# Causal mask of the first scores added by VectorE in PSUM instead of by matmuls; later pairs' q evacuated by ScalarE instead of VectorE

## The reference

```python
xn = layernorm(x)                                   # x: 8 x 2048 x 1024, one sequence per core
q, k, v = split(xn @ W_attn + b_attn)               # 16 heads of 64
att = (q @ k.T) / sqrt(64) / temperature
att = where(k_pos <= q_pos, att + slope[h] * (k_pos - q_pos), -inf)
y = softmax(att) @ v
h = silu(xn @ wg.T / 127) * (xn @ wu.T / 127)       # 3072 wide
out = x + (y @ W_proj + b_proj) + h @ wd.T / 127
```

## Time and profile before

| | |
|---|---|
| median of 3 runs | 1139.33 us (1138.94 to 1139.5) |
| profiled execution | 1137.8 us |
| its span on the slowest core (core 2) | 1136.2 us; the other cores 1131.2 to 1134.5 us |
| mean granted TensorE clock | 0.997 on that core |
| TensorE, VectorE, ScalarE, GpSimd busy | 1082.9, 628.3, 479.5, 332.8 us |

### The profile page before, as it was taken

The page is one execution under the profiler, slowest core; times in us unless marked ns, Lnnn a source line. Parts: engine busy times, 40 slices in busy tenths (PEclk is TensorE's granted clock), DMA queues, the critical chain, the costliest instruction groups (busy, mean ns, idle before and its releaser), DMA issues.

```text
span 1136.2 us, 23969 instructions; the slowest of 8 cores (1131.2 to 1136.2 us)
## 1 busy us (share of the span) xinstructions
PE 1082.9 (95%) x7270; PEld 535.8 (47%) x7270; DVE 628.3 (55%) x1254; ACT 479.5 (42%) x869; POOL 332.8 (29%) x529
## 2 busy tenths in 40 slices
PE   2898899999999999999999999999999999999998
PEld 1444355545545555454554554455554344444443
DVE  4531867776776786787777678677882100001100
ACT  2443345655655565555565556556666200000000
POOL 7210112423332342233333233223333422222220
PEclk9999999999999999999999999999999999999999
DMA  8448032433412433143331213113521552525222
GB/s 191 141 93 169 16 62 67 79 72 71 84 41 65 84 81 67 39 85 67 71 57 33 64 38 67 32 33 69 173 61 54 203 190 74 185 74 185 74 77 72
DMA packets 57070, 98.34 MB, mean 87 GB/s; under 512 B 23292, under 2 KB 43909, under 8 KB 55862
## 3 DMA queue, kind: packets, MB, share of 16 engines
q0 software_dynamic: 7872, 35.66, 16.1%
q1 hardware_dynamic: 46178, 52.65, 15.7%
q10 hardware_dynamic: 2900, 8.51, 1.9%
HBM read 90.50 MB, written 27.26 MB: 104 GB/s over the span
## 4 chain that ended last, share of the span: by engine, by line
PE 87%; DVE 6%; issue 3%; DMA 2%; ACT 1%; POOL 1%; DVEq 0%; ACTq 0%; POOLq 0%; SPq 0%
PE ps_gu L752 25%; PE ps_dn L914 15%; PE ps_s L843 10%; PE ps_t L824 10%; PE ps_m L732 9%; PE ps_y L862 5%; PE ps_dn L909 5%; PE ps_t L792 5%; DVE cm L577 3%; PE ps_s L846 1%; DMA xstage<-xin 1%; DVE hst L513 1%; DMA tile_s<-tiles 1%; DVE qx L607 1%; DVE st L525 0%
## 5 line engine op out<-in xcount | busy, mean ns | idle before, releaser
L694 ACT ACTIVATE pt<-ps_t 128x512 bf16<-128x512 f32 (+1 forms) x576 | 328.6, 575 | 297.9 <-PE ps_t L824 283.2
L577 DVE TENSOR_REDUCE cm<-ps_s 128x1 f32<-128x512 f32 (+3 forms) x640 | 377.1, 607 | 136.4 <-PE ps_s L843 81.6
L752 PE MATMUL ps_gu<-xnT,wubuf 128*128 128x512 bf16 x768 | 261.5, 378 | 2.3 <-DVE hst L513 2.3
L752 PE MATMUL ps_gu<-xnT,wgbuf 128*128 128x512 bf16 x768 | 261.8, 378 | 1.2 <-ACT kst L638 1.2
L843 PE MATMUL ps_s<-kx,qx 67*128 67x512 bf16 (+3 forms) x640 | 215.6, 347 | 12.9 <-DVE cm L577 9.2
L824 PE MATMUL ps_t<-qx,kx 104*128 104x512 bf16 (+3 forms) x640 | 212.6, 348 | 5.2 <-DVE qx L607 4.4
L914 PE MATMUL ps_dn<-wdres,hb 128*128 128x512 bf16 x768 | 168.5, 379 | 0.0
L443 POOL TENSOR_SCALAR th_s<-th_s 128x512 f32<-128x512 f32 x96 | 59.4, 619 | 364.6 <-ACT th_s L646 364.0
L862 PEld LDWEIGHTS ps_y<-Vt,pt 128*128 128x128 bf16 x2176 | 121.5, 97 | 79.3 <-issue 0.9
L627 DVE SCALAR_TENSOR_TENSOR outsb<-ps_dn,xres 128x512 f32<-128x512 f32 x32 | 20.7, 687 | 205.1 <-PE ps_dn L914 205.1
L862 PE MATMUL ps_y<-Vt,pt 128*128 128x65 bf16 x2176 | 134.1, 193 | 0.0
(11 more groups left out here) (75 smaller groups left out, 707.9 us busy)
## 6 DMA issues: line engine op xcount, KB each, us to landing
h_sc<-hst SPq DMA_DIRECT2D x96, 128.0 KB, 1.9
hb<-h_sc SPq DMA_DIRECT2D x4, 3072.0 KB, 14.3
xstage<-xin SPq DMA_DIRECT2D x16, 512.0 KB, 6.2
xres<-xin POOLq DMA_DIRECT2D x16, 512.0 KB, 4.9
out<-outsb ACTq DMA_DIRECT2D x15, 512.0 KB, 3.0
wgbuf<-wg_r POOLq DMA_DIRECT2D x12, 512.0 KB, 5.3
wubuf<-wu_r POOLq DMA_DIRECT2D x12, 512.0 KB, 7.9
wd_sc<-wd_r POOLq DMA_DIRECT2D x12, 512.0 KB, 7.7
```

What stands on the lines that cost most here:

```text
L577: e.tensor_reduce(cm[:, c0:c0 + 1], ps_s[:, s % 2 * 512:s % 2 * 512 + w], AX.X, AluOpType.max, negate=True).then_inc(sem["v_mx"], 1)
L694: e.activation(pt[t % NPT][:, 0:w], ps_t[:, t % 2 * 512:t % 2 * 512 + w], AF.Exp).then_inc(sem["a_e"], 1)
L752: mm = e.matmul(ps_gu[:, r // 8 * 512:r // 8 * 512 + 512], w[:, w0:w0 + 128], xnT[:, dc * T + tb * 512:dc * T + tb * 512 + 512], start=(dc ...
```

## The change

The mask matmuls go. VectorE instead adds `mask_s` to the last 128 columns of a diagonal group, in place in PSUM, and reduces the group when that addition has told of its end through a new semaphore `v_ms`. The evacuation of q for pairs 1 to 7 moves from VectorE (one `tensor_scalar`) to ScalarE (one `activation`, same scale and bias); pair 0 stays. SyncE and TensorE wait for ScalarE's semaphore `a_q` there.

```diff
@@ block.vector, reduces of a step
                     e.wait_ge(sem["p_s"], s + 1)
+                    if part == b:
+                        d0 = s % 2 * 512 + w - 128
+                        e.tensor_tensor(ps_s[:, d0:d0 + 128], ps_s[:, d0:d0 + 128], mask_s[:, 0:128],
+                                        AluOpType.add).then_inc(sem["v_ms"], 1)
+                        e.wait_ge(sem["v_ms"], 4 * n + i + 1)
                     e.tensor_reduce(cm[:, c0:c0 + 1], ps_s[:, s % 2 * 512:s % 2 * 512 + w], AX.X,
                                     AluOpType.max, negate=True).then_inc(sem["v_mx"], 1)
@@
-                if M is not None and M[0] == "qk" and M[2] and M[1] % 2 == 0:
-                    evac_q(M[1] // 8 + 1, M[1] % 8 // 2)
@@ block.scalar
+            def evac_q(p, tc):
+                e.wait_ge(sem["p_qk"], 8 * p + 2 * tc + 1)
+                e.wait_ge(sem[f"l_h{(p - 1) % 2}{tc}"], (96 if tc == 0 else 64) * ((p - 1) // 2 + 1))
+                if p == 1 and tc == 0:
+                    e.wait_ge(sem["v_cbq"], 1)
+                e.activation(qst[:, tc * 512:(tc + 1) * 512], ps_m[:, :], AF.Identity, bias=cbq_s[:, p:p + 1],
+                             scale=cvec_s[:, :]).then_inc(sem["a_q"], 1)
@@
-                if M[0] == "qk" and M[2] and M[1] % 2:
-                    evac_k(M[1] // 8 + 1, M[1] % 8 // 2)
+                if M[0] == "qk" and M[2]:
+                    (evac_k if M[1] % 2 else evac_q)(M[1] // 8 + 1, M[1] % 8 // 2)
@@ block.tensor
-                    diag = c0 == b * 512
-                    mm = e.matmul(ps_s[:, r0:r0 + w], q_[0:KS, b * 512 + i * 128:b * 512 + (i + 1) * 128],
-                                  k_[0:KS, c0:c0 + w], start=True, stop=not diag)
-                    if diag:
-                        mm = e.matmul(ps_s[:, r0 + w - 128:r0 + w], ident_s[:, :], mask_s[:, 0:128],
-                                      start=False, stop=True)
-                    mm.then_inc(sem["p_s"], 1)
+                    e.matmul(ps_s[:, r0:r0 + w], q_[0:KS, b * 512 + i * 128:b * 512 + (i + 1) * 128],
+                             k_[0:KS, c0:c0 + w], start=True, stop=True).then_inc(sem["p_s"], 1)
@@ block.sync, shift (in block.tensor, m_free names the same semaphore)
+                elif p:
+                    e.wait_ge(sem["a_q"], 4 * (p - 1) + tc + 1)
```

More of the change, by code:

```diff
@@ L42 @@
     "g_set", "g_sel", "g_th", "g_s", "g_xr",
-    "v_t", "v_cbq", "v_ln", "v_xn", "v_q", "v_mx", "v_mc", "v_m", "v_rc", "v_y", "v_h", "v_out",
-    "a_c", "a_sd", "a_xe", "a_v", "a_k", "a_e", "a_th", "a_g", "a_b",
+    "v_t", "v_cbq", "v_ln", "v_xn", "v_q", "v_ms", "v_mx", "v_mc", "v_m", "v_rc", "v_y", "v_h", "v_out",
+    "a_c", "a_sd", "a_xe", "a_v", "a_k", "a_q", "a_e", "a_th", "a_g", "a_b",
     "p_c", "p_xT", "p_v", "p_qk", "p_s", "p_m", "p_t", "p_av", "p_g", "p_u", "p_b", "p_d", "p_dl",
@@ L310, in build_program @@
                     n_q += 1
-                    m_users.append(("v_q", n_q))
+                    m_users.append(("a_q", n_q - 4))
         def pair_done(p):
@@ L328, in shift @@
                     e.wait_ge(sem["a_k"], 4 * p + tc + 1)
+                elif p:
+                    e.wait_ge(sem["a_q"], 4 * (p - 1) + tc + 1)
                 else:
-                    e.wait_ge(sem["v_q"], 4 * p + tc + 1)
+                    e.wait_ge(sem["v_q"], tc + 1)
                 for j in range(2):
@@ L498, in _, with evac_q @@
         def _(e):
[L499 to L502, removed]
+            def evac_q(tc):
+                e.wait_ge(sem["p_qk"], 2 * tc + 1)
                 e.tensor_scalar(qst[:, tc * 512:(tc + 1) * 512], ps_m[:, :], cvec_s[:, :],
-                                cbq_s[:, p:p + 1], AluOpType.mult, AluOpType.add).then_inc(sem["v_q"], 1)
+                                cbq_s[:, 0:1], AluOpType.mult, AluOpType.add).then_inc(sem["v_q"], 1)
             def gate_times_up(f):
@@ L549, in _ @@
                 if i >= 6 and i % 4 == 2:
-                    evac_q(0, i // 4 - 1)
-            evac_q(0, NTB - 1)
+                    evac_q(i // 4 - 1)
+            evac_q(NTB - 1)
             y_due = []
```

## The result

The changed kernel takes 1166.37 us in the median (1165.14 to 1168.39), the one before 1139.13 beside it: a ratio of 1.0245, with a 95% interval of 1.0228 to 1.0261, or +27.9 us. The forecast was 1154, slower by 15, within 1136 to 1168; of the loss it had about half. Some executions of the kernel before and of some experiments ran in a second, slower state of the chip, and the ratios leave them out; `mask_h0_evac` kept only two, has no ratio, and was run again.

What follows compares the result with a forecast made beforehand. TensorE was taken as the bound, often stopped by VectorE's reduce. Seven pairs 11 us, last pair 3, fill 1: +15, including the removed 14.3, gives 1152.8; the median's 1.5 more gives 1154 (range 1136 to 1168; own 1146 to 1163, chance 0.55).

Steps and rivals of the forecast that it cites:

- a dearer step: Rival on VectorE's masked reduces: 0.46 to 0.50 us per add from a slower PSUM write, 1161 to 1165 us; chance 0.17.
- a late ScalarE: Rival: q in front of exponentials delays ps_y and ps_t, up to 14 us on top, 1160 to 1168 us; chance 0.03.
- Direction and mechanism: Attention stage: slower, chance 0.75; adds delay VectorE's reduces, and TensorE's scores wait for a half, bunched in blocks 0 and 1.
- The add's price: VectorE, 256 adds of 128 columns: 0.29 us each, its reduce 0.40 us behind the add's start, 102 us in all.
- The estimate of 0.46 us by the other page: VectorE's add into PSUM: 0.46 us each if PSUM cost the overhead difference, about 125 ns against 60; unused in the forecast.
- q on ScalarE at nothing: 28 q evacuations at 0.78 us on ScalarE, 22 us, fit its idle time and were costed at nothing.
- the ledger: Delays from longer reduces carried through the trace of one pair of heads and summed over the attention stage: +15 us.
- How the loss grows with the step: Whole kernel, by VectorE time per add: -5 us at 0.20, +6 at 0.30, +15 at 0.40, +21 at 0.46.
- TensorE's waits grow by about 29 us: Attention stage: with the removed 14.3 us of mask matmuls inside the +15 us sum, TensorE's added waits for VectorE.
- the fill at the start 1 us: Start of the attention stage, VectorE busy 29.6 of 37 us: adds cost 1 us in the sum.
- the last pair behaves twice like the first head, 3 us: Last pair of heads, without projections: each head loses like the first head of the traced pair, 3 us together.
- Seven such pairs: The pairs of heads before the last: each ends 1.6 us behind like the traced one, 11 us in all.

Runs made afterwards that it cites:

- mask_h0_evac: Kernel before with mask matmuls in head 0 alone, none replaced, q of pairs 1 to 7 on ScalarE: 1124.58 and 1125.43 us; run again, 1126.06 us.
- add_b01: The full change in blocks 0 and 1 only, mask matmuls kept in blocks 2 and 3: ratio 1.0187 to the kernel before.
- add_b23: The full change in blocks 2 and 3 only, mask matmuls kept in blocks 0 and 1: ratio 1.0042 to the kernel before.
- add_free: Changed kernel, but the add writes its own SBUF tile and the reduce doesn't wait for it; head 0 keeps mask matmuls: 1143.96 us, ratio 1.0056.
- evac_only: Changed kernel with mask matmuls put back and the add taken out, so only q moves to ScalarE: 1135.4 us, ratio 0.9978 to the kernel before.
- add_sbuf: Changed kernel, but the add writes to SBUF and the reduce still waits for it; head 0 keeps mask matmuls: 1164.56 us, ratio 1.0231.
- run 24: Not a run or kernel: the words belong to "scores run 24 groups ahead", where run is a verb; no time or ratio belongs to it.
- add_pair0: The full change's adds in the first pair of heads alone, mask matmuls elsewhere, later q on ScalarE: ratio 1.0038 to the kernel before.
- add_pair7: The full change's adds in the last pair of heads alone, mask matmuls elsewhere, q of pairs 1 to 7 on ScalarE: ratio 1.003.
- mask_h0: Kernel before without the mask matmuls of heads 1 to 15, nothing in their place, q on VectorE: 1128.9 us, ratio 0.9923.
- after: The changed kernel itself, with the add in PSUM and q on ScalarE: 1166.37 us, ratio 1.0245 to the kernel before.

## Why the prediction came out as it did

**The number: half luck.** 1166.4 lies in the range of 1136 to 1168 but above the forecast's own 1146 to 1163. The upper end was put there for a dearer step and for a late ScalarE, and neither came: the step was 0.39 to 0.40 us and q cost nothing. What filled that room was counted nowhere, as said below.

**Direction and mechanism: right.** TensorE lost what VectorE's reduce took longer, through the two halves of `ps_s`, and mostly in blocks 0 and 1: `add_b01` against `add_b23`.

**The add's price: right.** 0.296 us against 0.29 taken from the 128-column reduce; 0.39 to 0.40 between starts against 0.40. The rule that the semaphore costs nothing extra (the Trainium skill, VectorE: DVE Perf Modes, "The DRAIN you can't avoid") would have had the kernel near `add_free`. It took 20 us more, so the trace was the one to follow. The estimate of 0.46 us by the other page (the Trainium skill, Perfetto Trace Analysis, "Optimizing Scalar/DVE Operations"), if a PSUM destination cost what VectorE's overhead differs by there, doesn't hold here: 296 against 288 ns.

**q on ScalarE at nothing: right**, by `evac_only`; it took 777 ns each against 0.78. Its gain was in the ledger, with no price of its own.

**How the loss grows with the step: right.** The ledger had -5 us for a step of 0.20 and +15 for 0.40. `add_free` and `add_sbuf` stand at +6 and +26. The slope is the forecast's, 20 us; both kernels stand 11 us above it.

**The step that failed: "TensorE's waits grow by about 29 us".** They grew by 43. I took the distances between starts of matmuls in the stage, less the columns at 2.4 GHz, wherever more than 20 ns were left: 37 us on the slowest core before, 80 after. (Of the 80, 5.5 lie where the granted clock was 0.50, and are in part slower columns and not waits.) The ledger took one pair of heads as a sample of the stage, and it was no fair one. By the table the forecast lacks some 12 us, in three places:

- "the fill at the start 1 us". The first two heads took 5.1 us where the sum had 2.6, 4.4 of it in the first. There scores run 24 groups ahead with few other matmuls between, and VectorE sets the pace alone, so an add is paid nearly in full: 16 adds at 0.40 us are 6.4, and the head lost 4.4 and the 0.9 that its mask matmuls took. `add_pair0` has the same 4.5.
- "the last pair behaves twice like the first head, 3 us". It took 6.9; `add_pair7` has 6.4 of it alone. The stretch has no projections between the scores, as said, but the first head of pair 2 was no measure for that.
- "Seven such pairs". The six in the middle took 14.8 us where 9.6 were counted. They range from 1.4 to 3.8. The pair of the ledger itself took 3.3, not 1.6.

The ledger also had TensorE at 2.4 GHz throughout, as before the change. On three cores, the slowest among them, pair 1 took another 1.7 us at the lower clock, which no term of the sum held; the table's median leaves most of it out.

In the ledger's own pair, from unit 16's first score to unit 20's, all cores took 2.7 to 2.8 us longer, where the ledger had 1.5. The timeline above begins with a cast of four columns (L602) that takes 1.13 us; in the kernel before it took 0.17 there. GpSimd's row at that time, in the changed kernel:

```profile
307.07 1.15 POOL L451 TENSOR_TENSOR gs_s<-th_s,gh_s 128x512 bf16<-128x512 f32 x1 [0.27 <-POOL th_s L445]
```

The cast ends with GpSimd's step, at 308.25 against 308.22, on all eight cores. The Trainium skill, SBUF — State Buffer, "Who interferes with whom", has VectorE and GpSimd share a pair of ports by an exclusive lock for a whole instruction, and the trace agrees as far as that one ends with the other. The kernel before has six such casts of over 0.5 us and the changed one four, one of them at the same place; so they aren't more. This one stood in front of unit 16's four adds. What it cost TensorE isn't shown: unit 16 took 1.26 us longer, and the same unit of pairs 4, 6 and 7 took 1.03, 1.08 and 1.10 longer with a cast of 0.17 in front of it. Another one can be followed further, in pair 1:

```profile
259.76 0.92 DVE L602 CAST nm<-cm 128x4 bf16<-128x4 f32 x1 [0.17 <-DVE cm L582]
260.98 0.70 DVE L610 TENSOR_TENSOR qx<-ps_m,tile_s 8x512 bf16<-8x512 f32 x1
261.82 0.38 PE L835 MATMUL ps_t<-qx,kx 104*128 104x512 bf16 x1 [1.56 <-DVE qx L610]
```

VectorE has no wait between that cast and L610, and TensorE stands 1.56 us for L610. In the kernel before it stood 0.19 us at this place. By these rows the 0.75 us that the cast took longer went on to TensorE there. No run took a collision away, so their share is read from the rows only. What makes the middle pairs dearer than counted is otherwise open. The 32 mask matmuls that each pair saves were worth 1.2 us and not 1.8 in `mask_h0`, which may be a part of it.

## What to carry to other kernels

Where two engines trade halves of a buffer, price a moved step by the time between starts of dependent steps in the trace, not by its duration, and multiply it only where no idle time stands before it: the same 128 adds cost 24 us in the dense blocks and 7 in the others. A stage of unlike stretches needs a ledger for each: the start, the repeated middle and the end here took 4.4, 1.4 to 3.8 a pair, and 6.9 us. Before moving masking work, ask whether it is needed: a maximum that softmax cancels need not be masked where the bias is mild, and leaving out 240 masks was worth more than either place to put them. Head 0 is the one with the steepest slope, 0.707 by position, which adds up to 90 to the score of a masked key 127 positions ahead of its query; its masks stayed in every version here.

## What the runs showed of the hardware

**The clock fell where TensorE waited for VectorE.** Windows of the changed kernel (columns as in the earlier trace rows):

```profile
111.00:115.00 4.00, 2.62 (x13) 1.00 (x11) 1.28 (x3) 0.69 (x1) 0.00 (x0) 1.00 0.28 72
115.00:119.00 4.00, 3.27 (x9) 0.76 (x9) 3.41 (x11) 0.00 (x0) 0.00 (x0) 0.69 0.07 19
119.00:123.00 4.00, 3.86 (x10) 1.24 (x11) 3.21 (x8) 2.37 (x3) 1.65 (x2) 0.50 0.00 0
123.00:127.00 4.00, 3.18 (x16) 1.12 (x14) 3.49 (x10) 0.81 (x2) 0.11 (x1) 0.96 0.00 0
```

TensorE's granted clock is 0.50 from about 116 to 123 us, the 1.2 GHz level, after a stretch in which it waited for the first masked reduces between its matmuls. All eight cores show it in the changed kernel, for 3.4 or 6.8 us, and none after 105 us in the kernel before or in `mask_h0`. It costs little there, since VectorE sets the pace: in `add_sbuf` two cores kept the full clock and took 41.8 us for the first head, and those that lost it 42.0 to 42.3. With 4.4 us lost in that head, the clock has at most some 0.5 of it.

Where TensorE sets the pace the same 3.4 us cost half their length. In pair 1 the clock fell again on cores 2, 6 and 7, and not on the others. Core 7 in that stretch, and core 1 at the same place of the program:

```profile
263.30:266.70 3.40, 3.40 (x14) 1.40 (x12) 2.44 (x5) 1.19 (x2) 0.00 (x0) 0.50 0.11 39
261.00:264.40 3.40, 3.40 (x24) 1.68 (x22) 3.19 (x7) 1.24 (x3) 0.00 (x0) 1.00 0.11 39
```

TensorE did 14 matmuls instead of 24, and pair 1 took 1.7 us longer on these three cores (5.3 against 3.6). On both cores TensorE had just stood 1.56 us for L610 behind the long cast of 259.76, so the rows don't show why one clock fell and the other stayed. The time is that of the slowest core, and core 7 was the slowest.

**A step on VectorE that needs the one before it** starts 0.10 us after its end, and one that doesn't 0.08 before it (128 columns from PSUM): 0.38 to 0.40 against 0.21 us between starts. The 0.39 is the same with the result in PSUM (`after`) and in SBUF (`add_sbuf`).
